# Graph network kernel: encoder three blocks earlier, two chunks normalized on ScalarE, three parts of a fifth sum in the counting stage

## What is computed

```python
h = relu(layernorm(x))                              # 3125 x 128
h = relu(h @ enc_w1.T + enc_b1) @ enc_w2.T + enc_b2 # encoder
for w in conv_w:                                    # 5 layers
    agg = segment_sum((h @ w)[src], dst)
    gi, gh = agg @ wih.T + bih, h @ whh.T + bhh     # GRU
    r, z = sigmoid(ir + hr), sigmoid(iz + hz)
    h = (1 - z) * tanh(i_n + r * h_n) + z * h
x = x + sigmoid(relu(relu(h) @ dec_w1.T + dec_b1) @ dec_w2.T + dec_b2)
# second network: layernorm, two sums with degree scales around a 128-256-128 MLP
```

## Time and profile before

| | us |
|---|---|
| runs | 757.24, 756.96, 758.71 |
| median | 757.24 |
| profiled execution | 759.16 |
| its span, first to last instruction | 755.9 |
| TensorE busy | 724.1 |
| VectorE busy | 335.6 |
| ScalarE busy | 311.6 |

### The profile page before, as it was taken

One profiled execution on the slowest core, in us unless ns is written; L12 is line 12 of the kernel. 1 busy time (PEld: TensorE's weight loads), 2 busy tenths in 40 slices (PEclk: granted clock), 3 DMA queues, 4 the chain that ended last, 5 costly groups with the idle time before them and its releaser, 6 DMA issues.

```text
span 755.9 us, 9898 instructions
## 1 busy us (share of the span) xinstructions
PE 724.1 (96%) x4074; PEld 396.4 (52%) x4074; DVE 335.6 (44%) x681; ACT 311.6 (41%) x453; POOL 39.4 (5%) x55
## 2 busy tenths in 40 slices
PE   2789999999999999999999999999999999999997
PEld 2556666444444444444444444544444545567886
DVE  7999998533212233122341222656644721125222
ACT  2788777744423445233463333432446421221000
POOL 5120000000000000000000000120011310000000
PEclk9999999999999999999999999999999999999999
DMA  6020000823402124021140212520002000000000
GB/s 181 6 74 1 2 1 1 139 50 60 62 1 47 38 46 80 1 47 38 37 89 1 48 36 37 91 84 2 1 0 103 1 1 1 1 1 10 30 24 30
DMA packets 78795, 28.40 MB, mean 38 GB/s; under 512 B 70340, under 2 KB 77893, under 8 KB 78618
## 3 DMA queue, kind: packets, MB, share of 16 engines
q1 hardware_dynamic: 77786, 26.93, 17.0%
q0 software_dynamic: 240, 0.66, 0.3%
q10 hardware_dynamic: 720, 0.13, 0.1%
HBM read 8.03 MB, written 2.60 MB: 14 GB/s over the span
## 4 chain that ended last, share of the span: by engine, by line
PE 83%; DVE 11%; ACT 2%; DMA 1%; issue 1%; POOL 1%; SPq 1%; ACTq 0%; DVEq 0%
PE PSA L1174 36%; PE PSA L1386 8%; PE PSA L1255 5%; PE PSA L1331 5%; DVE CT L821 4%; PE PSA L1188 3%; PE PSA L1197 3%; PE PSA L1190 3%; PE PSA L1192 3%; PE PSA L1196 3%; PE PSA L1199 3%; PE PSA L1120 3%; PE PSA L1319 2%; PE PSA L1307 1%; DVE stat L786 1%; ACT AT L1493 1%
## 5 line engine op out<-in xcount | busy, mean ns | idle before, releaser
L1174 PE MATMUL PSA<-AT,H 128*128 128x512 fp8e3 (+1 forms) x1522 | 287.1, 348 | 0.8 <-DMA H<-H 0.6
L1174 PEld LDWEIGHTS PSA<-AT,H 128*128 128x128 f16 x1522 | 131.6, 98 | 158.6 <-issue 13.6
L1015 DVE SCALAR_TENSOR_TENSOR rS<-PSA,bias,rS 128x512 f32<-128x512 f32 (+1 forms) x35 | 23.9, 682 | 269.2 <-ACT rS L1550 269.2
L1550 ACT ACTIVATE rS<-PSA,bias 128x512 f32<-128x512 f32 (+1 forms) x35 | 22.1, 632 | 203.0 <-PE PSA L1196 203.0
L821 DVE TENSOR_TENSOR CT<-CT 128x2048 bf16<-128x2048 bf16 x80 | 91.2, 1204 | 0.0
L1493 ACT ACTIVATE AT<-PSA 128x1000 fp8e3<-128x1000 f32 (+1 forms) x79 | 74.3, 997 | 29.3 <-PE PSA L1120 29.3
L1467 ACT ACTIVATE CTL<-AT 128x3125 fp8e3<-128x3125 fp8e3 (+1 forms) x25 | 69.9, 2797 | 0.0
L1386 PE MATMUL PSA<-AT,CT 128*128 128x256 f16 x576 | 66.6, 277 | 0.8 <-DVE AT L987 0.8
L1331 PE MATMUL PSA<-CT,H 128*128 128x512 fp8e3 (+1 forms) x336 | 65.5, 351 | 1.2 <-POOL H L731 1.2
L1386 PEld LDWEIGHTS PSA<-AT,CT 128*128 128x128 fp8e3 x576 | 56.4, 100 | 8.2 <-DVE AT L987 0.9
L1120 PE MATMUL PSA<-CT 128*128 128x125 bf16 x625 | 47.3, 230 | 12.7 <-DVE CT L821 11.1
(11 more groups left out here) (169 smaller groups left out, 648.7 us busy)
## 6 DMA issues: line engine op xcount, KB each, us to landing
AT<-scale_scratch SPq DMA_DIRECT2D x1, 1562.5 KB, 6.4
H<-in_x SPq DMA_DIRECT2D x1, 1536.0 KB
out<-AT SPq DMA_DIRECT2D x12, 128.0 KB
comb_scratch<-CT SPq DMA_DIRECT2D x1, 960.0 KB, 5.9
comb<-comb_scratch SPq DMA_DIRECT2D x5, 192.0 KB, 2.9
H<-yS SPq DMA_TRANSPOSE x48, 2.5
H<-in_x SPq DMA_DIRECT2D x1, 512.0 KB, 4.9
CT<-AT SPq DMA_TRANSPOSE x25, 3.9
```

The lines of the kernel that those rows point to most:

```text
L1174: last = nc.tensor.matmul(bank[:, 0:w], H16[:, l % 2, t, h, :], AT3[:, t, n0:n0 + w], start=(t == 0 and h == 0), stop=(t == T - 1 and (h = ...
```

## The change

`ENC` goes from 2 to -1, so that the encoder begins ahead of block 0, and with it move `KEYS_AT`, `COMB` and `PART`. The encoder's step 0 is called once ahead of the loop. Chunks 0 and 1 are normalized by ScalarE, with scale and bias (`lnsc`, `lnb`) and Relu; the bias is a new small step of VectorE, `shifts`. Chunks 2 to 6 stay on VectorE, under a semaphore of their own. The statistics of chunk 2 and later run one block earlier. GpSimd takes the powers of chunks 0 and 1 between its gathers rather than behind all five. The parts of sums 0 to 3 are placed up to three blocks earlier, and blocks 37 to 39 take the parts of source chunks 0 to 2 of sum 4; its other parts run in the main loop.

```diff
-        ENC = 2
-        KEYS_AT = {4: 1, 10: 2, 16: 3, 23: 4}
+        ENC = -1
+        KEYS_AT = {5: 1, 11: 2, 17: 3, 23: 4}
-        PART = {16: (0, 4), 18: (0, 5), 20: (0, 6)}
-        PART.update({8 + 2 * g: (0, g) for g in range(4)})
-        PART.update({17: (1, 0), 19: (1, 1)})
...
+        PART = {7: (0, 0), 8: (0, 1), 9: (0, 2), 14: (1, 0), 16: (1, 1)}
+        PART.update({5 + 2 * g: (0, g) for g in range(3, NC)})
...
+        PART.update({37 + g: (4, g) for g in range(NBT - 37)})
+        BEGUN = NBT - 37
+        COMB = [2 + l for l in range(L)]
...
+            gathered(0)
+            gathered(1)
+            roots(0)
+            gathered(2)
+            roots(1)
+            gathered(3)
+            gathered(4)
...
+            def shifts(s):
+
+                t0, nt = CH[s]
+                dve.wait_ge(roots_ready, s + 1)
+                nc.vector.scalar_tensor_tensor(lnb[:, t0:t0 + nt], mv[:, t0:t0 + nt, 0], -1.0, lnsc[:, t0:t0 + nt],
+                                               ALU.mult, ALU.mult).then_inc(shifts_ready, 1)
...
             first_norm(0)
             keys(0)
+            shifts(0)
             first_norm(1)
...
+                if b == 0:
+                    shifts(1)
+                if b % 2 == 1 and (b + 3) // 2 < NC:
+                    first_norm((b + 3) // 2)
                 if b % 2 == 0 and 2 <= b // 2 + 1 < NC:
-                    first_norm(b // 2 + 1)
+                    normalized(b // 2 + 1)
                 off = b - ENC
-                if off >= -2 and off % 2 == 0 and (off + 2) // 2 < NC:
-                    normalized((off + 2) // 2)
...
-                    pe.wait_ge(state_encoded, (1, 4, NC, NC)[k - 1])
+                    pe.wait_ge(state_encoded, (3, 6, NC, NC)[k - 1])
...
+                if g == 0 and q == 4:
+                    pe.wait_ge(sum_copied, 1)
...
             transposed_keys(0)
+            encoder(0)
...
-                    if AHEAD <= q:
+                    if q == AHEAD:
+                        for g in range(BEGUN, NC):
+                            aggregate_part(q, g)
+                    if AHEAD < q:
...
+            def normalized(s):
+
+                t0, nt = CH[s]
+                act.wait_ge(shifts_ready, s + 1)
+                for t in range(t0, t0 + nt):
+                    k = rows(t)
+                    last = nc.scalar.activation(X32[0:k, t, :], X32[0:k, t, :], ACT.Relu, bias=lnb[0:k, t:t + 1],
+                                                scale=lnsc[0:k, t:t + 1])
+                last.then_inc(tile_normalized, 1)
...
             copied_keys(0)
+            normalized(0)
+            encoder(0)
             for b in range(NBT):
                 windows(b)
+                if b == 0:
+                    normalized(1)
```

More of the change, by code:

```diff
@@ L236, in gnn_kernel @@
         AHEAD = 4
-        ENC = 2
-        KEYS_AT = {4: 1, 10: 2, 16: 3, 23: 4}
+        ENC = -1
+        KEYS_AT = {5: 1, 11: 2, 17: 3, 23: 4}
         assert all(b + 1 < k * (PW // J) for b, k in KEYS_AT.items())
-        PART = {16: (0, 4), 18: (0, 5), 20: (0, 6)}
-        PART.update({8 + 2 * g: (0, g) for g in range(4)})
-        PART.update({17: (1, 0), 19: (1, 1)})
[L243 to L247, removed]
+        PART = {7: (0, 0), 8: (0, 1), 9: (0, 2), 14: (1, 0), 16: (1, 1)}
+        PART.update({5 + 2 * g: (0, g) for g in range(3, NC)})
+        PART.update({16 + g: (1, g) for g in range(2, NC)})
+        PART.update({23 + g: (2, g) for g in range(NC)})
+        PART.update({30 + g: (3, g) for g in range(NC)})
+        PART.update({37 + g: (4, g) for g in range(NBT - 37)})
+        BEGUN = NBT - 37
+        COMB = [2 + l for l in range(L)]
+        assert max(PART) < NBT and len(PART) == AHEAD * NC + BEGUN
         EA, EB, EC2 = 6, 1, 7
@@ L269, in gnn_kernel @@
         variances_ready = sem("variances_ready"); roots_ready = sem("roots_ready")
-        tile_normalized = sem("tile_normalized"); scales2_ready = sem("scales2_ready")
+        shifts_ready = sem("shifts_ready"); tile_normalized = sem("tile_normalized"); later_normalized = sem("later_normalized"); scales2_ready = sem("scales2_ready")
         x_transposed = sem("x_transposed"); x_copied = sem("x_copied"); enc1_product = sem("enc1_product")
@@ L700, in _, with gathered @@
             pool.memset(mv[:, :, :], 1.0).then_inc(small_set, 1)
-            for k in range(KW):
+            def gathered(k):
                 pool.wait_ge(rows_found, k + 1)
@@ L706, in _, with roots @@
                                         ).then_inc(edges_gathered[k], 16)
-            pool.wait_ge(mhalf_set, 1)
[L708 to L711, removed]
+            def roots(n):
+                t0, t1 = CH[NORMS[n][0]][0], CH[NORMS[n][1] - 1][0] + CH[NORMS[n][1] - 1][1]
+                pool.wait_ge(variances_ready, n + 1)
+                pool.tensor_tensor(lnsc[0:P, t0:t1], mv[0:P, t0:t1, 1], mhalf[:, 0:1].to_broadcast([P, t1 - t0]), ALU.pow
+                                   ).then_inc(roots_ready, 1)
+            pool.wait_ge(mhalf_set, 1)
+            gathered(0)
[5 more added lines that the diff above has]
+            gathered(4)
+            for n in range(2, len(NORMS)):
+                roots(n)
             pool.memset(deg[:, :], 0.0).then_inc(small_set, 1)
@@ L832, in normalized @@
                                                    ALU.subtract, ALU.mult)
-                last.then_inc(tile_normalized, 1)
+                last.then_inc(later_normalized, 1)
             def low_encoded(s):
@@ L1135, in encoder @@
                     t0, nt = CH[s]
-                    pe.wait_ge(tile_normalized, s + 1)
+                    pe.wait_ge(tile_normalized, s + 1) if s < 2 else pe.wait_ge(later_normalized, s - 1)
                     if s >= 1:
```

## The result

| | before | after |
|---|---|---|
| runs, us | 757.24, 756.96, 758.71, 757.11 | 750.97, 750.52, 751.35, 750.25 |
| median | 757.17 | 750.75 |
| profiled execution | 759.16 | 750.97 |
| its span | 755.9 | 748.8 |

The ratio is 0.9908, with a 95% interval of 0.9895 to 0.9921: faster by 0.8 to 1.1%. The forecast was 751.0.

What follows compares the result with a forecast made beforehand. VectorE's queue bounds the counting stage first, then TensorE's own work. Closing 1.0 us sooner plus 5.2 us of the fifth sum done makes 6.2 off 757.24: 751.0 us, range 750.0 to 753.6.

Steps and rivals of the forecast that it cites:

- What bounds the stage: Counting stage: VectorE's queue bounds it until block 12's comparisons at 57.26, TensorE's own work from 59.56 on.
- VectorE's queue: Ahead of block 18: two normalizations leave, 2.04 us less; two shifts add 0.16 each, the last low half 0.28.
- Waiting for x: VectorE's statistics of chunk 2, behind block 1, wait for the second load of x: 0.15 us, outer bound 2.3.
- Where TensorE takes over: In the new order TensorE catches up with VectorE just before block 18, whose counts start at 75.5.
- The tail: TensorE from block 18 to the stage's close: 55.57 - 3.9 + 5.2 = 56.9 us, ending at 132.4.
- The sum: Stage closes 1.0 us sooner with 5.2 us of the fifth sum already done: together 6.2 us.
- one of the signs that I had named against the prediction: VectorE waiting for the high halves in the changed profile would make the prediction wrong.
- After the stage: Chunk 3's gate products come 5.2 us sooner; copy of sum 3 and sync queue leave room, so all shifts alike.
- given back in layer 0: Sync queue or ScalarE paces chunks 3 to 5, the 5.2 us become waits, 1.0 is left: 756.2; chance 0.07.
- The other sign that I had named: A new wait of TensorE between 150 and 200 us would make the prediction wrong.
- The lower clock: Rival: TensorE stays at 1.2 GHz in the early stage; lasting until 60 us it makes 760.8; chance 0.05.
- Its own base: The 6.2 us were taken off 757.24, the median of the runs shown, giving 751.0; the profiled run took 759.16.

Runs made afterwards that it cites:

- The early and the late work on VectorE: Changed kernel plus three unused VectorE additions of 512 columns, behind the comparisons of block 10 (752.8 us) or of block 36 (751.67 us).
- the second profile: Profile from timing the unmodified changed kernel again with more rounds: median 752.02 us, stage closing at 132.08.
- the just filled gap: Changed kernel plus 9 unused fp32 matmuls of 128 columns on TensorE behind block 5, in the wait ahead of block 6: 752.5 us.

## Why the prediction was right

**What bounds the stage: right.** The early and the late work on VectorE lie on the two sides of the turning point, and at the stage's end they cost 1.78 and 0.01 us, as the theory of each had it.

**VectorE's queue: right in kind, too small by 0.5 us.** Taking the two normalizations out, shifts put in, gave 1.91 us (kernel before with that alone) and 1.93 (put back); the forecast had 2.04 less two shifts of 0.16, 1.72. It took normalizations by the distance of starts, 1.02 us, but the small instructions by their durations: a shift is followed after 0.07 us, not 0.16, and the last low half after 0.20 (78.91 to 79.11 before, 68.83 to 69.03 after), not 0.28. Waiting for x: none, forecast 0.15. One small wait was overlooked, VectorE's for a high half in the kernel before, which is gone in the second profile: a low half starts at 67.21, 0.20 us later than four comparisons from 62.52 on need. From the first comparisons to those of block 18 the queue took 59.36 us instead of 61.35, 1.99 less. My terms for that stretch give 1.45 (the first shift stands ahead of it), and these rows make up the rest. A term of the other sign was missing: GpSimd's first gather goes out at 7.40 instead of 6.77, so the first keys wait for their edges and all of the queue starts 0.34 us later. I had looked at the gathers behind the powers and not at the first one. Why it goes out later stays open; VectorE works out its row numbers at 6.25 in both.

**Where TensorE takes over: 75.70 and, without the low clock, 75.17; forecast 75.5.** The wait there is 0.28 and 0.59, where I had put about one.

**The tail: right.** 132.94 - 75.70 = 57.2 and 132.08 - 75.17 = 56.9, forecast 56.9; the rest of the fifth sum is 26 matmuls in 5.78 us.

**The sum: right, with one statement wrong and some luck.** The gain at the stage's end is 5.63 and 6.49 in the two profiles; forecast 6.2. Their difference is the low clock in block 6, which the forecast didn't have. That 751.0 came within 0.25 of the median is luck: the late first keys and the small terms cancel to 0.3 us, the layer edges keep some tenths, and the runs of the result lie at the lower of the two levels; the second series has a median of 752.02. I wrote that a delay in the first blocks is paid back in waits up to block 18 "and costs nothing unless VectorE itself is stopped". It was stopped: in the first profile VectorE waits for a high half of ScalarE, one of the signs that I had named against the prediction, though of 0.39 us only. The second profile doesn't show it.

```profile
64.23 0.69 DVE L862 SCALAR_TENSOR_TENSOR H<-PSA,H 128x512 f16<-128x512 f32 x1 [0.39 <-ACT H L1574]
```

**After the stage: nearly all kept.** At 690 us the gain is 5.4 of 5.63 in the first profile and 5.9 of 6.49 in the second; the edge at 483 us takes some, with new waits of 0.33 and 0.67 us for the state's transposes, where before had none. The other sign that I had named, a new wait of TensorE between 150 and 200 us, is there with 0.18 us at 191.83. The rival "given back in layer 0" is real as a mechanism at a tenth of its size or less, and with 1.1 us where one transpose is slow (the just filled gap).

**The lower clock: the rival's way of working is there, not its size.** The rise came at 19 to 21 instead of 28.8, by itself some microseconds of TensorE's time, but in a stretch where VectorE paces it, so little of it shows at the end. What I hadn't foreseen is that the level can fall again in the middle of the stage. The Trainium skill, "TensorE: Matmul & The Clock Gate", Part 1, has the low level as the default that activity lifts; the falls after a wait agree with that, though the same wait of 2.08 us was followed by full speed in most traces.

**Its own base.** I took 6.2 off the median and not off the profiled 759.16. That was the better choice for a reason that I didn't know: the profiled execution of before had the slow tail, the one of after hadn't, and of the 7.1 us between the spans 1.66 are that row.

## What to carry to other kernels

Find in the chain of waits the point where the bound passes from one engine to another: here work on the first engine counted in full ahead of it and not at all behind it, and two small probes, one on each side, measured that. An engine that is slower at a piece of work is the better place for it when the faster one sets the pace and the slower one has time. In a queue of small instructions take costs from the distance of starts and not from durations: the shift lasted 0.15 us and cost 0.07. And before two profiles are subtracted, look for rows of equal work with different durations: here one row of 24 matmuls would have passed for 1.66 of 7.1 us of gain.

## What the hardware showed

- TensorE's clock falls back to 1.2 GHz for one stretch after a wait, in some executions and not in others of the same kernel: behind the wait of 2.09 us ahead of block 6 in light work in three of ten traces (3.6 us at the low level in the first, 0.86 at the stage's end), and behind waits of 0.66, 0.17 and 0.75 us in the tail in seven of twelve (4.46 us instead of 2.80 for 24 matmuls). The tail makes two levels of run time 1.7 us apart. The kernel before has two such levels as well (757.1 and 758.8), and its one trace, of 759.16, has 4.46. With matmuls that nobody reads in the tail's waits no run was at the upper level.
- The mean granted clock shows these falls (0.54, 0.62), but not the slow start: it reads 1.00 in 15.40 to 28.84 of before, where durations are those of 1.2 GHz.
- GpSimd's power on 128 x 4 took 1.03 us on its own before and 1.9 in the changed kernel's later calls; the profile shows no engine that waited for it:

```profile
10.29 1.04 POOL L714 TENSOR_TENSOR lnsc<-mv,mhalf 128x4 f32<-128x4 f32 x1 [0.47 <-DVE mv L813]
...
13.60 1.96 POOL L714 TENSOR_TENSOR lnsc<-mv,mhalf 128x4 f32<-128x4 f32 x1 [0.99 <-DVE mv L813]
```

- A DMA transpose that takes 1.55 us as a rule takes 2.3 to 2.9 once between 170 and 520 us, at a place that moves with the program. Where it lands ahead of a layer edge it costs 1.1 us.
